# Three small DMAs of a split bias, moved from before the barrier that ends the setup to behind it

## The reference, cut to what matters

```python
x = x + xattn0(layernorm(x), ctx)        # one head, q/k/v projections, softmax over 375 rows
x = x + ffn0(layernorm(x))               # 3 blocks: linear, layernorm, gelu, linear, residual
x = x + xattn1(ctx, layernorm(x))        # 16 heads
x = x + ffn1(layernorm(x))               # ternary weights, quantised activations
```

## Time and profile before

| | us |
|---|---|
| median of three runs | 1260.29 (1260.25 to 1265.25) |
| the profiled execution's own time | 1259.43 |
| its span, from the first to the last instruction | 1257.7 |
| PE busy | 1071.7 (85% of the span) |
| DVE busy | 864.7 (69%) |
| ACT busy | 526.7 (42%) |
| POOL busy | 510.5 (41%) |
| mean granted TensorE clock | 0.946 of full speed |

### The profile page before, as it was taken

The page is one execution under the profiler, slowest core; times in us unless marked ns, Lnnn a source line. Parts: engine busy times, 40 slices in busy tenths (PEclk is TensorE's granted clock), DMA queues, the critical chain, the costliest instruction groups (busy, mean ns, idle before and its releaser), DMA issues.

```text
span 1257.7 us, 30813 instructions
## 1 busy us (share of the span) xinstructions
PE 1071.7 (85%) x9234; PEld 773.5 (62%) x9234; DVE 864.7 (69%) x2318; ACT 526.7 (42%) x953; POOL 510.5 (41%) x879
## 2 busy tenths in 40 slices
PE   6479999999999698989896579999999999766665
PEld 5357777777777566566654237666666666534444
DVE  4365566566556357676765578888889888468887
ACT  3212222222222211111112436666666665568886
POOL 1126444444444122222210133455555544566664
PEclk8689999999999899999998869999999999869998
DMA  8512333332223100000001697778877887550001
GB/s 221 154 58 67 92 92 92 90 88 85 87 86 92 28 1 1 0 0 0 1 1 40 145 159 153 157 161 162 160 157 158 160 158 152 169 159 26 25 25 34
DMA packets 121106, 116.08 MB, mean 92 GB/s; under 512 B 44867, under 2 KB 114022, under 8 KB 121062
## 3 DMA queue, kind: packets, MB, share of 16 engines
q1 hardware_dynamic: 121062, 115.54, 39.2%
HBM read 79.15 MB, written 36.00 MB: 92 GB/s over the span
## 4 chain that ended last, share of the span: by engine, by line
PE 48%; DVE 22%; issue 10%; SPq 6%; ACT 5%; DMA 3%; POOL 3%; DVEq 1%; POOLq 0%; ACTq 0%
PE bank L1514 26%; DVE nm L1300 7%; PE bank L1672 6%; PE bank L1608 3%; DVE hT L1219 2%; PE bank L1784 2%; PE bank L1597 2%; PE bank L1860 2%; DVE yn L1208 2%; PE bank L1754 2%; ACT v_all L1019 1%; PE bank L1770 1%; POOL rs L713 1%; ACT v_all L1014 1%; DVE v_all L1399 1%
## 5 line engine op out<-in xcount | busy, mean ns | idle before, releaser
L1300 DVE TENSOR_REDUCE nm<-bank 112x1 f32<-112x375 f32 x512 | 247.0, 537 | 14.9 <-PE bank L1754 14.4
L962 ACT ACTIVATE pT<-bank 125x448 f32<-125x448 f32 x384 | 184.9, 543 | 55.2 <-PE bank L1770 54.7
L1754 PE MATMUL bank<-ks,qs 96*128 96x375 bf16 x512 | 167.1, 337 | 23.3 <-DMA qs<-q_parts_dram 18.4
L1770 PE MATMUL bank<-qs,ks 128*128 128x112 bf16 x1536 | 137.7, 213 | 0.6 <-DMA qs<-mrow 0.6
L1770 PEld LDWEIGHTS bank<-qs,ks 128*128 128x128 bf16 x1536 | 111.8, 99 | 21.6 <-DMA qs<-mrow 0.8
L1784 PE MATMUL bank<-pT,vaug 125*32 125x112 f32 x3072 | 100.1, 263 | 0.0
L913 ACT ACTIVATE yT<-bank,bcol,gcol 128x448 f32<-128x448 f32 x48 | 32.2, 721 | 160.3 <-PE bank L1654 160.3
L1672 PE MATMUL bank<-wffT,hT 128*112 128x256 f32 x384 | 98.9, 391 | 0.0
L1514 PE MATMUL bank<-wv1T,ctxT 128*125 128x256 f32 x384 | 88.0, 379 | 0.0
L1514 PE MATMUL bank<-ctxT,wk1T 128*128 128x375 f32 x256 | 87.6, 485 | 0.0
L1784 PEld LDWEIGHTS bank<-pT,vaug 125*32 125x32 f32 x3072 | 69.2, 109 | 24.1 <-issue 16.9
(11 more groups left out here) (204 smaller groups left out, 2294.1 us busy)
## 6 DMA issues: line engine op xcount, KB each, us to landing
k_parts_dram<-kp SPq DMA_DIRECT2D x192, 93.8 KB, 3.5
ks<-k_parts_dram SPq DMA_DIRECT2D x64, 281.2 KB, 4.2
cnat<-in_ctx_dram SPq DMA_DIRECT2D x32, 375.0 KB
ks<-k_parts_dram SPq DMA_DIRECT2D x64, 187.5 KB, 3.9
ks<-k_parts_dram SPq DMA_DIRECT2D x64, 93.8 KB, 3.3
q_parts_dram<-qp SPq DMA_DIRECT2D x48, 112.0 KB, 2.2
qs<-q_parts_dram SPq DMA_DIRECT2D x64, 84.0 KB, 4.0
x_stream<-in_x_dram SPq DMA_DIRECT2D x4, 896.0 KB, 13.2
```

The source lines that it names most:

```text
L962: act.activation(pT[:, u % 6, :], B3[u % 3][0:TP], ACT.Exp).then_inc(probs_made, 1)
L1300: dve.tensor_reduce(nm[:, h:h + 1], A3[h % 3][0:L], AX_X, ALU.max, negate=True).then_inc(head_max_taken, 1)
L1754: mm(A3[h % 3], qs[par][0:KS, h * L:h * L + P], ks[par][0:KS, h * T:(h + 1) * T], start=True, stop=True).then_inc(max_scores_made, 1)
L1770: last = mm(B3[c][:, j * L:(j + 1) * L], ks[par][:, h * T + c * TP:h * T + c * TP + P], qs[par][:, h * L:(h + 1) * L], start=True, stop=True)
```

## The change

```diff
             for n in range(1, 4):
                 load_x(n)
 
-            sp.wait_ge(bias_parts_made, 3)
+            stage_end(sp, "sp", 1)
+
+
             for s in range(3):
                 sp.dma_start(b1parts[s:s + 1], b1p[0:1, s]).then_inc(bias_parts_in_place, 16)
-            sp.wait_ge(bias_parts_in_place, 48)
-            stage_end(sp, "sp", 1)
 
 
             sp.dma_start(wd[0], w1T[:, :, :].rearrange("p k n -> p (k n)")).then_inc(ternary_w_stored, 16)
             sp.dma_start(wd[1], w2T[:, :, :].rearrange("p c n -> p (c n)")).then_inc(ternary_w_stored, 16)
+            sp.wait_ge(bias_parts_in_place, 48)
 
             def store_k(b, par, n):
                 sp.wait_ge(k_part3_made, b + 1)
```

## The result

| | before | changed |
|---|---|---|
| median, us | 1260.27 (4 runs, 1256.99 to 1265.25) | 1247.43 (4 runs, 1243.07 to 1249.62) |
| ratio of times | | 0.9893, 95% interval 0.9868 to 0.9919 |
| profiled execution's own time | 1259.43 | 1243.07 |
| its span | 1257.7 | 1241.3 |
| mean granted TensorE clock | 0.946 | 0.951 |

The change made the kernel 12.8 us faster by these medians. The changed kernel was run again on two other chips: 1248.67 against 1257.59 (8.9 us, ratio 0.9925, 0.9909 to 0.9941) and 1247.35 against 1258.86 (11.5 us, ratio 0.9908, 0.9896 to 0.9921). The mean of the three differences is 11.1 us, the sum that was forecast; as each of them is uncertain by two or three us, an agreement to a tenth is luck.

The account below looks back on a forecast made before the run. SP's issue and landing of three moves ahead of the barrier were taken to bound the kernel, by order, not work. All other terms taken as 0, 1260.3 - 11.1 = 1249.2 us; range for 8 in 10 1245.5 to 1254.

Parts of the forecast that it names:

- The barrier: Barrier ahead of stage 1: without the moves SP drains at 43.52, TensorE starts at 43.8 instead of 54.89, 11.1 us gained.
- The drain: SP's drain at the barrier with three x loads in flight: cost taken as 0, bounds 0 and 10.5 us.
- both rivals that hung on it: SP's drain waits for data (1259.7 us, chance 0.08) or until the queue has taken what was issued (1253.0, chance 0.06).
- The moves behind the barrier: SP's three moves beside TensorE's first batch: issue 5.08 us, landing 54.6, cost 0 while covered, cover 6.6 us.
- The contexts: Context loads of batches 0 and 1, needed earlier by TensorE: cost taken as 0, at the worst 3.0 us.
- DVE's wait for x: DVE's statistics move from 70.45 to 59.3, the last x load lands at 54.0: cover 5.3 us, cost 0.
- Computing beside full queues: Batch 0 runs while x lands: operations might stretch, some 0.3 us on DVE; taken as 0.
- The clock: TensorE starts stage 1 at the lower level again: taken as 0, bounds 4.9 us gained and some 2 us lost.
- The slower rival: TensorE's stalls and clock drops fall otherwise in the whole run, mean clock 0.920: 1266.6 us, chance 0.05.

Follow-up runs that it names:

- e1_wait_only: Against the kernel before: only the wait for the three moves' landing goes behind the barrier, their issue stays ahead; 1253.82 against 1258.58 us.
- e3_no_moves: The changed kernel without the three moves and the wait for them, so the bias of ffn0's first linears is left out; 1247.49 us.
- e2_wait_at_end: The changed kernel with SP's wait for the three moves at the end of stage 1 instead of ahead of the loop; 1247.70 us.
- e4_many_moves: The changed kernel with 42 moves of 1.5 KB behind the barrier instead of 3; 1253.89 against 1258.58 us of the kernel before.
- e8_quiet_pool: Against the changed kernel: early loads, DVE splits the bias in an earlier gap, POOL waits for DVE's ternary weights and normalises batch 1 behind the barrier; 1241.15 us.
- e7_all_early: Against the changed kernel: contexts loaded earlier, SP arrives directly behind them, POOL splits the bias instead of DVE, bias columns awaited at stage 1's end; 1247.02 us.
- e6_keep_warm: The changed kernel with 36 transposes of the identity behind TensorE's last weight job, filling its wait at the barrier; 1246.30 us.
- e9_pool_beside: The changed kernel with 12 extra products of 112x256 on POOL, beside DVE's unpacking of the quantised weights; 1251.50 us.

## Why the prediction was right

The median fell by 12.8 us in the first comparison and by 11.1 in the mean of three; 11.1 was forecast. The mechanism is shown, since TensorE's start, reckoned from the end of the x issue, moved by the issue and the landing less 0.12 us for the drain; the tenth in the medians is luck. Stage 1, forecast to end at 411.5, ended at 409.2, 411.7 and 409.6. Point by point:

1. *The barrier.* Right in mechanism and size. SP's arrival is set by its last x issue, POOL is nearly level with it, 0.4 to 0.7 us ahead (forecast 0.2). TensorE's start was put at 43.8 and measured at 42.15, 43.42 and 42.59: the setup's own length varies by that much, and I had taken one execution's 43.48 as fixed.
2. *The drain.* Taken as 0, measured 0.13 us with three loads in flight and 0.37 in e1_wait_only. It is more than the 7 ns of the earlier trace rows, but both rivals that hung on it (10.5 us of waiting for data, 3.8 for the queue) are excluded.
3. *The moves behind the barrier.* Right: e3_no_moves and e2_wait_at_end gain nothing over the change. The wait ended at 53.4 and the buffer was released at 58.9, a cover of 5.4 us where I gave 6.6. The load's lead over its use, which I named without a size, adds some 6, and e4_many_moves showed that a wait there is partly one that TensorE would have had anyway.
4. *The contexts.* Taken as 0, kept at 3.0. No wait names them at 42.15, nor at 40.92 in the profile of e4_many_moves. When they landed no profile shows, as nobody waited.
5. *DVE's wait for x.* DVE began its statistics at 57.05 without waiting; the last load of x, issued at 38.35, landed 14.5 us later, at 52.9. Cover 4.2 us.
6. *Computing beside full queues.* DVE's copy took 0.39 us beside them, as in the earlier trace rows. Right. The pair of POOL rows that I used there (1.44 and 0.72 us) had another lesson that I passed over: the long one lay beside DVE's split (39.40 to 40.65), and in e8_quiet_pool, where the split is gone from there, both took 0.73. It was the contention that later cost e7_all_early its gain.
7. *The clock.* It fell between 41 and 43 us in the three profiles and the batch was slow again, as taken. The window of the slow part was shorter than before, batch 0 took 14.19, 13.65 and 14.30 us against 14.86; this 0.6 to 1.2 us was inside my bounds. The bound of 4.9 us for a batch at the upper level was measured at 3.9 by e6_keep_warm.

The slower rival needed the mean granted clock to fall to 0.920; it was 0.951, 0.947 and 0.951. What stays open: where in stages 2 to 4 the 3 us from one execution to the next arise, and when the contexts had landed.

## What to carry to other kernels

Put ahead of a barrier only what the next stage reads: three tiny transfers there cost their issue behind the bulk loads (4.5 to 5 us) and the landing of the last (6.6 us), and every engine waited for both. Before moving work to an idle engine, look at who runs beside it, since POOL at work nearly doubled the time of DVE's operations here and ate most of a gain of 6 us. A change at a barrier is best read from the start of the next stage, since the span has 3 us of its own.

## What the runs showed of the hardware that was not expected

- VectorE's products of 128x256 f32 took 0.42 us alone and 0.73 to 0.75 beside GpSimd's, its int32 to f32 conversions of 128x512 took 0.42 and 0.77 to 0.91 (e7_all_early, e9_pool_beside); GpSimd's products of 112x256 took 0.61 alone and 0.80.
- SP's drain doesn't wait for transfers in flight: 0.13 us with three loads of 896 KB under way, the last of which landed 11 us later (the changed kernel), against 0.007 with none.
- What a DMA issue costs depends on what was issued just before: the first move took 2.7 to 3.8 us right behind the x loads, the next two 0.6 to 1.3. Issued 4.8 us after the x loads' issue had ended, the first took 0.60 (e9_pool_beside). The landing of the third came 6.6 us after its issue behind the x loads, against 1.71 for the last of 42 when these had long landed (e4_many_moves).
